# A graph network's gather-max scan: two columns a step fetched row by row into two turn buffers, instead of one and a quarter fetched into the ring

## The chip, the core and the metric

The kernel runs on one core of a Trainium2 chip. The core has five engines with a queue of instructions each: TensorE (PE), VectorE (DVE), ScalarE (ACT), GpSimd (POOL) and SyncE (SP). SyncE, ScalarE and GpSimd issue DMAs, which 16 DMA engines carry out. The metric is the device time of one execution in microseconds (us), lower is better.

## The reference, cut to what matters

Three graph layers on 6250 nodes with 200,000 edges, sorted by destination. Every layer takes, for each node, the maximum over the feature rows of its edges' sources, and projects it.

```python
def _sage_conv(x, src, dst, Wl, bl, Wr):
    agg = jax.ops.segment_max(x[src], dst, num_segments=x.shape[0])
    agg = jnp.where(jnp.isfinite(agg), agg, 0.0)
    return agg @ Wl + bl + x @ Wr
...
h = jnp.maximum(_layernorm(x, axis=-1), 0.0)
# three times, with the widths 128 -> 256 -> 256 -> 128:
h = jax.nn.leaky_relu(_sage_conv(h, src, dst, Wl, bl, Wr), 0.01)
return x + h
```

## The kernel before, in words

**Data.** The edges are cut into 512 runs of 391: 4 chains in each of 128 partitions. A *column* is one edge of one chain in all 128 partitions, 128 feature rows of w numbers (w = 128 in layer 0, 256 in layers 1 and 2). Four columns, one of each chain, are a *group*; two groups are a *block* of 8 columns; seven blocks are the *ring*, 56 columns in the on-chip memory (SBUF). A *step* is one lap of the ring. Each layer has 27 full steps (0 to 26) and a last one of 52 columns.

**GpSimd** gathers the columns: one indirect DMA each (L448), which takes 128 row numbers from `stage` and fetches 128 rows of the layer's feature table. Before each block it waits (L441, L443) until VectorE has staged that block's row numbers and until the block's old content has been written to the log.

**VectorE** (`scan_step`) runs over the groups in order: the running maximum of the last group plus a restart term goes to PSUM (a sum, L758), then the maximum of that and the gathered group goes back into the ring (L792). At the first group of each block it also copies the row numbers of the block before it, for the next lap, to `stage` (L739) and counts `block_scanned` up. At the first group of a step this is the last block's numbers, and the count tells too that the last group of the step before is no longer read.

**SyncE** (`log_step`) writes every scanned group to a log in HBM, one store a group: L1240 after `group_scanned`, L1246 after `block_scanned`. The log is gathered from at the layer's end.

**Rows.** A column that GpSimd need not gather is fetched by 128 small DMAs instead, one row each, issued by SyncE and ScalarE. The row's place in the table is a register; a portion of rows begins with one register load (TENSOR_LOAD, L321) that reads that many numbers from `row_at`. Before, 160 rows a step are fetched so: the ring's last column and 32 partitions of the one before it. GpSimd gathers that one for 96 partitions. SyncE fetches 72 in nine portions of 8 (L1231) behind its stores, ScalarE 88 in eight portions of 11 (L1155) in one go. Both wait for the store of the ring's last block, since the rows land in the ring. VectorE waits for all of them before the last group's maximum.

**ScalarE** also carries the layer's own projections (`keep_pair`, a pair of tiles a step in steps 0 to 22, two more pairs afterwards): it copies TensorE's transposed tile (L1109), loads the next tile (`h_in`, L1104), and copies TensorE's product (L1118), after the step's rows. In layer 0 it counts run ends there as well (L1125 to L1131). The order of all work is written out by hand; semaphores alone tie the queues. After a layer's scan GpSimd gathers each node's row from the log, and TensorE and VectorE project and store.

## Time and profile before

| | us |
|---|---|
| median of 3 runs (6050.76 to 6064.11) | 6052.55 |
| the profiled execution, its own time | 6050.56 |
| its span, first to last instruction | 6048.9 |
| GpSimd busy | 4524.8 (75%) |
| VectorE busy | 2893.5 (48%) |
| TensorE busy | 732.5 (12%) |
| ScalarE busy | 225.4 (4%) |
| gathers of layers 0, 1, 2: from, to | 32 to 1956, 2037 to 3958, 4044 to 5965 |

Busy times do not count DMA issues, register loads and waits, so those of SyncE and ScalarE say little about how full their queues are; the timeline shows their DMA issues (SPq, ACTq), and the view of one source line shows the register loads. "Issue" is idle time in which an engine waits for nothing that the profile shows. Releasers are inferred from semaphores.

### The profile page before, as it was taken

What the parts mean: (1) busy time and instruction counts of PE and PEld (TensorE: products, weight loads), DVE (VectorE), ACT (ScalarE), POOL (GpSimd) and SP (SyncE); (2) the same over time, 40 slices, a digit from 0 to 9 for tenths busy, and PEclk for the clock granted to TensorE, in tenths of its full rate; (3) what the DMA queues carried; (4) which work ended last, traced back from release to release, by engine and by line L of the source; (5) the groups of instructions that cost most, each with busy time, mean ns of one, the idle gap of its engine ahead of it and who ended that gap; (6) DMA issues with size and microseconds to landing.
All of it is one profiled execution on the core that took longest, in us unless ns stands there. A gap on an engine that the chain in (4) does not pass through costs nothing.

```text
span 6048.9 us, 53349 instructions
## 1 busy us (share of the span) xinstructions
PE 732.5 (12%) x2214; PEld 411.8 (7%) x2214; DVE 2893.5 (48%) x3638; ACT 225.4 (4%) x664; POOL 4524.8 (75%) x4793
## 2 busy tenths in 40 slices
PE   1111111111100311111111110040010000100003
PEld 0000000000000200000000000030000000000002
DVE  5333333333333555555555555565555555555556
ACT  1000000000000100000000000010000000000001
POOL 6777777777777777777777777767777777777776
PEclk7555555555555655555555555575555555555556
DMA  4333333333333566666666666666666666666665
GB/s 141 108 111 107 108 108 109 110 108 108 108 108 107 171 216 218 218 216 220 216 218 218 216 219 214 215 206 219 217 220 215 218 218 216 220 215 218 215 216 175
DMA packets 461123, 1089.10 MB, mean 180 GB/s; under 512 B 116295, under 2 KB 181740, under 8 KB 461068
## 3 DMA queue, kind: packets, MB, share of 16 engines
q0 software_dynamic: 203520, 519.10, 30.6%
q1 hardware_dynamic: 220508, 544.04, 24.8%
q10 hardware_dynamic: 37040, 25.45, 1.5%
q14 instruction: 48, 0.39, 0.0%
q8 instruction: 7, 0.11, 0.0%
HBM read 555.08 MB, written 533.07 MB: 180 GB/s over the span
## 4 chain that ended last, share of the span: by engine, by line
POOL 49%; issue 17%; DMA 1%; POOLq 1%; DVE 0%; PE 0%; DVEq 0%
POOL ring L448 47%; POOL ring L475 2%; POOLq L444 0%; DMA ring<-running_max_log,end_row 0%; POOLq L441 0%; DMA patch<-running_max_log,patch_row 0%; DMA ring<-features,stage 0%; DMA running_max_log<-patch 0%; POOL patch L465 0%; DVE z_sum L902 0%; DVE agg L894 0%; POOLq L455 0%; POOLq L443 0%; DMA features<-h_out 0%; DVE patch L873 0%
## 5 line engine op out<-in xcount | busy, mean ns | idle before, releaser
L448 POOL DMA_INDIRECT ring<-features,stage x4611 | 4360.0, 946 | 1432.2 <-issue 1383.7
L792 DVE TENSOR_TENSOR ring<-banks,ring 128x1024 f32<-128x1024 f32 (+1 forms) x1173 | 1227.4, 1046 | 2954.0 <-DMA ring<-features,stage 2918.9
L758 DVE TENSOR_TENSOR banks<-ring,banks 128x1024 f32<-128x1024 f32 (+1 forms) x1173 | 1232.1, 1050 | 37.5
L975 PE MATMUL banks<-wr,h_turned 128*128 128x256 f32 (+1 forms) x490 | 220.7, 596 | 3623.4 <-ACT h_turned L1109 3623.4
L975 PEld LDWEIGHTS banks<-wr,h_turned 128*128 128x128 f32 x490 | 127.2, 320 | 3687.4 <-ACT h_turned L1109 3678.6
L991 PE MATMUL banks<-dst_low,own 128*128 128x394 bf16 x200 | 100.4, 502 | 976.0 <-DVE own L734 976.0
L475 POOL DMA_INDIRECT ring<-running_max_log,end_row x147 | 142.9, 972 | 65.6 <-issue 43.9
L1109 ACT ACTIVATE h_turned<-banks 128x256 f32<-128x256 f32 (+1 forms) x147 | 51.8, 353 | 3128.6 <-issue 2664.1
L739 DVE COPY stage<-edges 128x8 int32 (+1 forms) x588 | 119.4, 203 | 88.0 <-DVE banks L758 32.8
L977 PE MATMUL banks<-b,ones 1*128 1x256 f32 (+1 forms) x294 | 157.6, 637 | 0.0
L1048 PE MATMUL banks<-wl,agg 128*128 128x256 f32 (+1 forms) x490 | 110.7, 369 | 1.2 <-DVE agg L894 0.9
L992 PE MATMUL banks<-dst_high,own 128*128 128x394 bf16 x200 | 99.1, 496 | 0.0
L991 PEld LDWEIGHTS banks<-dst_low,own 128*128 (+1 forms) x200 | 27.8, 139 | 1023.0 <-issue 1021.8
L967 PE MATMUL banks<-ident,h_in 128*128 128x128 f32 x245 | 86.6, 436 | 27.8 <-DMA h_in<-features 27.8
L1125 ACT ACTIVATE signs<-banks,node 128x391 bf16<-128x391 f32 x50 | 29.6, 592 | 1505.5 <-issue 1501.8
L1048 PEld LDWEIGHTS banks<-wl,agg 128*128 128x128 f32 x490 | 84.3, 210 | 11.1 <-DVE agg L894 4.0
L977 PEld LDWEIGHTS banks<-b,ones 1*128 1x128 f32 x294 | 72.9, 307 | 74.4 <-issue 74.4
L1175 ACT ACTIVATE agg<-zeros 128x512 f32<-128x512 f32 x75 | 47.3, 631 | 761.1 <-PE banks L1048 761.1
L1017 PE MATMUL banks<-ident,ring 128*128 128x128 f32 x20 | 5.0, 425 | 577.8 <-DVEq L804 577.8
L1036 PE MATMUL banks<-ident,ring 128*128 128x128 f32 x245 | 59.2, 319 | 62.7 <-DMA ring<-running_max_log,end_row 59.0
L1118 ACT ACTIVATE own<-banks 128x256 f32 (+3 forms) x147 | 51.1, 348 | 394.0 <-PE banks L977 394.0
L883 DVE TENSOR_SCALAR finite<-banks 128x512 int32<-128x512 int32 (+2 forms) x75 | 44.3, 591 | 42.1 <-PE banks L1036 41.2
(114 smaller groups left out, 523.4 us busy)
## 6 DMA issues: line engine op xcount, KB each, us to landing
running_max_log<-ring SPq DMA_DIRECT2D x782, 512.0 KB, 3.1
running_max_log<-ring SPq DMA_DIRECT2D x391, 256.0 KB, 2.2
ring<-features ACTq DMA_DIRECT2D x4752, 1.0 KB
ring<-features,stage POOLq DMA_INDIRECT x4611, 3.2
ring<-features SPq DMA_DIRECT2D x3888, 1.0 KB
ring<-features ACTq DMA_DIRECT2D x2376, 0.5 KB
ring<-features SPq DMA_DIRECT2D x1944, 0.5 KB
h_in<-features ACTq DMA_DIRECT2D x98, 128.0 KB, 2.5
```

What stands on the lines that cost most here:

```text
L448: pool.indirect_dma_start(ring[0:rows, c * w:(c + 1) * w], None, tables[l], bass.IndirectOffsetOnAxis(ap=stage[0:rows, b, u:u + 1].bitcast ...
L475: pool.indirect_dma_start(ring[:, t * w:(t + 1) * w], None, logs[w], bass.IndirectOffsetOnAxis(ap=end_row[:, t:t + 1].bitcast(U32), axis=0 ...
L739: dve.tensor_copy(stage[:, b, :], src_t[:, bass.ds((i + ahead) * RING_COLS + b * BLOCK_COLS, BLOCK_COLS)]).then_inc(block_scanned, 1)
L758: dve.tensor_tensor(sum_ps[:, 0:CHAINS * w].rearrange("p (h f) -> p h f", h=CHAINS), group(g - 1).rearrange("p (h f) -> p h f", h=CHAINS), ...
L792: dve.tensor_tensor(group(g), sum_ps[:, 0:CHAINS * w], group(g), ALU.max).then_inc(turn, 1)
L967: turn = pe.transpose(turn_ps[0][:, c * P:(c + 1) * P], h_in[p][:, c * P:(c + 1) * P], ident[:, :])
L975: pe.matmul(mm_ps[p][:, 0:n], h_turned[p][:, c, :], wr_sb[l][:, c, :], start=(c == 0), stop=False)
L977: pe.matmul(mm_ps[p][:, 0:n], ones[0:1, :], b_sb[l][:, :], start=False, stop=True).then_inc(own_mm, 1)
L991: pe.matmul(sel_ps[p][:, 0:RUN + 3], chosen, dst_low[:, h, :], start=(h == 0), stop=False)
L992: mm = pe.matmul(sel_ps[p][:, 0:RUN + 3], chosen, dst_high[:, h, :], start=False, stop=(h == CHAINS - 1))
L1036: turn = pe.transpose(turn_ps[b][:, t * w + c * P:t * w + (c + 1) * P], ring[:, k * w + c * P:k * w + (c + 1) * P], ident[:, :])
L1048: mm = pe.matmul(mm_ps[b][:, t * n:(t + 1) * n], agg[b][:, t * w + c * P:t * w + (c + 1) * P], wl_sb[l][:, c, :], start=(c == 0), stop=(c ...
```

## The change

- **Rows.** 256 rows a step are fetched row by row, two whole columns (`FETCHED_COLS`). They go to two new buffers, `fetched0` and `fetched1`, used in turn by step, not to the ring. GpSimd gathers 54 columns a step.
- **Shares.** SyncE fetches 128 rows in eight portions of 16, ScalarE 128 in four of 32. Both may start a step's rows once `block_scanned` says that VectorE is in the step before; the wait for the store of the last block goes. SyncE fetches portion 0 before the first store, then two after each store until all are issued.
- **Stores.** One store for a block in place of two, but in the last step of a layer.
- **Last group.** VectorE takes its maximum in two instructions: the two gathered columns first, then, after the wait for the rows, the two fetched ones.
- **ScalarE.** In layers 1 and 2 a step's own projections stand between the four portions, not behind them.
- **Loops.** VectorE, SyncE and ScalarE loop over two steps at a time, for the two buffers; step 0, and on ScalarE four steps at the end, are written out. Some semaphores are merged.

```diff
-SYNC_ROWS, SYNC_AT_ONCE = 72, 8
-ACT_AT_ONCE = 11
-ROWS = 160
+FETCHED_COLS = 2
+SYNC_ROWS = 128
+AT_ONCE, ACT_AT_ONCE = 16, 32
...
+    ROWS = FETCHED_COLS * P
...
-        return width(b, last) - (b == BLOCKS - 1 and not last)
+        return width(b, last) - (FETCHED_COLS if b == BLOCKS - 1 and not last else 0)
...
+        fetched = [sb(f"fetched{k}", [P, FETCHED_COLS * F_MAX]) for k in range(2)]
...
-                            rows = 2 * P - ROWS if c == RING_COLS - 2 and not last else P
                             pool.indirect_dma_start(
-                                ring[0:rows, c * w:(c + 1) * w], None, tables[l],
+                                ring[:, c * w:(c + 1) * w], None, tables[l],
                                 bass.IndirectOffsetOnAxis(
-                                    ap=stage[0:rows, b, u:u + 1].bitcast(U32), axis=0),
+                                    ap=stage[:, b, u:u + 1].bitcast(U32), axis=0),
                             ).then_inc(late_landed if last and b == LATE_BLOCK and u >= CHAINS else landed[b], DMA)
...
-                        elif g == GROUPS - 1:
-                            dve.wait_ge(act_rows_landed, FETCHED[1])
-                            dve.sem_inc(act_rows_landed, -FETCHED[1])
-                            dve.wait_ge(sync_rows_landed, FETCHED[0])
-                            dve.sem_inc(sync_rows_landed, -FETCHED[0])
                         dve.wait_ge(turn, carried + 2 * g + 1)
-                        dve.tensor_tensor(group(g), sum_ps[:, 0:CHAINS * w], group(g), ALU.max).then_inc(turn, 1)
+                        if g == GROUPS - 1:
+                            gathered = (CHAINS - FETCHED_COLS) * w
+                            dve.tensor_tensor(group(g)[:, 0:gathered], sum_ps[:, 0:gathered], group(g)[:, 0:gathered],
+                                              ALU.max).then_inc(turn, 1)
+                            dve.wait_ge(act_rows_landed[turn_of], FETCHED[1])
+                            dve.sem_inc(act_rows_landed[turn_of], -FETCHED[1])
+                            dve.wait_ge(sync_rows_landed[turn_of], FETCHED[0])
+                            dve.sem_inc(sync_rows_landed[turn_of], -FETCHED[0])
+                            dve.tensor_tensor(group(g)[:, gathered:CHAINS * w], sum_ps[:, gathered:CHAINS * w],
+                                              fetched[turn_of][:, 0:FETCHED_COLS * w], ALU.max).then_inc(turn, 1)
+                        else:
+                            dve.tensor_tensor(group(g), sum_ps[:, 0:CHAINS * w], group(g), ALU.max).then_inc(turn, 1)
...
-                def fetch_rows(i):
-
-                    act.wait_ge(group_scanned, i * BLOCKS + (FIRSTS * l + 1))
-                    if isinstance(i, int):
+                def rows_open(i):
+
+                    if isinstance(i, int) and i == 0:
                         act.wait_ge(rows_placed, len(widths))
-                        if l:
-                            act.wait_ge(logged[BLOCKS - 1], LOGGED[BLOCKS - 1] * l)
                     else:
-                        act.wait_ge(logged[BLOCKS - 1], i * (DMA * STORES_OF[BLOCKS - 1]) + LOGGED[BLOCKS - 1] * l)
-                    for first in range(0, ROWS_OF[1][1], ACT_AT_ONCE):
+                        act.wait_ge(block_scanned, i * BLOCKS + SIGNED * l)
+
+                def fetch_rows(i, turn_of, portions):
+
+                    for portion in portions:
+                        first = portion * ACT_AT_ONCE
                         places = row_places(1, mybir.EngineType.Activation, i, first, ACT_AT_ONCE, w)
                         for r, place in enumerate(places):
-                            act.dma_start(row_slot(1, first + r, w), table_row(l, w, place)
-                                          ).then_inc(act_rows_landed, DMA)
+                            act.dma_start(row_slot(1, turn_of, first + r, w), table_row(l, w, place)
+                                          ).then_inc(act_rows_landed[turn_of], DMA)
+
+                def step_of_rows(i, pair, turn_of):
+
+                    rows_open(i)
+                    if pair and l:
+                        for p in range(2):
+                            fetch_rows(i, turn_of, range(2 * p, 2 * p + 1))
+                            keep_turned(i, p, True)
+                            fetch_rows(i, turn_of, range(2 * p + 1, 2 * p + 2))
+                            keep_own(i, p)
+                    else:
+                        fetch_rows(i, turn_of, range(ACT_PORTIONS))
+                        if pair:
+                            keep_pair(i, 2)
 
                 load(0, 0)
                 load(1, 1)
-                fetch_rows(0)
-                keep_pair(0, 2)
-                with act.Fori(1, PAIRS - 2) as j:
-                    fetch_rows(j)
-                    keep_pair(j, 2)
-                with act.Fori(PAIRS - 2, PAIRS) as j:
-                    fetch_rows(j)
+                def two_steps(j, pair):
+
+                    step_of_rows(j * 2 + 1, pair, 1)
+                    step_of_rows(j * 2 + 2, pair, 0)
+
+                step_of_rows(0, True, 0)
+                with act.Fori(0, PAIRS // 2 - 1) as j:
+                    two_steps(j, True)
+                two_steps(PAIRS // 2 - 1, False)
                 keep_pair(PAIRS - 2, PAIR_TILES[-1])
                 keep_pair(PAIRS - 1, 0)
-                with act.Fori(PAIRS, STEPS - 1) as j:
-                    fetch_rows(j)
+                two_steps(PAIRS // 2, False)
...
-                def fetch_rows(i, g):
-
-                    first = g * SYNC_AT_ONCE
-                    if g == 0:
+                def fetch_rows(i, turn_of, portion):
+
+                    first = portion * AT_ONCE
+                    places = row_places(0, mybir.EngineType.SP, i, first, AT_ONCE, w)
+                    for r, place in enumerate(places):
+                        sp.dma_start(row_slot(0, turn_of, first + r, w), table_row(l, w, place)
+                                     ).then_inc(sync_rows_landed[turn_of], DMA)
+
+                def log_step(i, last, turn_of=0):
+                    portion, portions = 0, 0 if last else SYNC_ROWS // AT_ONCE
+                    if not last:
                         if isinstance(i, int):
                             sp.wait_ge(rows_placed, len(widths))
                             if l == 0:
@@ -1223,34 +1260,29 @@
                             else:
                                 for b in range(STORES):
                                     sp.wait_ge(h_stored[b], PER_OUT * l)
-                                sp.wait_ge(logged[BLOCKS - 1], LOGGED[BLOCKS - 1] * l)
                         else:
-                            sp.wait_ge(logged[BLOCKS - 1], i * (DMA * STORES_OF[BLOCKS - 1]) + LOGGED[BLOCKS - 1] * l)
-                    places = row_places(0, mybir.EngineType.SP, i, first, SYNC_AT_ONCE, w)
-                    for r, place in enumerate(places):
-                        sp.dma_start(row_slot(0, first + r, w), table_row(l, w, place)
-                                     ).then_inc(sync_rows_landed, DMA)
-
-                def log_step(i, last):
+                            sp.wait_ge(block_scanned, i * BLOCKS + SIGNED * l)
+                        fetch_rows(i, turn_of, portion)
+                        portion += 1
                     for b in used_blocks(last):
 
                         c, columns = b * BLOCK_COLS, width(b, last)
-                        if columns > CHAINS:
+                        if last and columns > CHAINS:
                             sp.wait_ge(group_scanned, i * BLOCKS + (FIRSTS * l + b + 1))
                             sp.dma_start(log_block(l, i, b, 0, CHAINS), ring[:, c * w:(c + CHAINS) * w]
                                          ).then_inc(logged[b], DMA)
-                            if not last and BLOCK_GROUPS * b * SYNC_AT_ONCE < SYNC_ROWS:
-                                fetch_rows(i, BLOCK_GROUPS * b)
                         sp.wait_ge(block_scanned, i * BLOCKS + (SIGNED * l + BLOCKS + b + 1))
-                        at = columns - CHAINS
-                        sp.dma_start(log_block(l, i, b, at, CHAINS), ring[:, (c + at) * w:(c + columns) * w]
+                        at = columns - CHAINS if last else 0
+                        sp.dma_start(log_block(l, i, b, at, columns - at), ring[:, (c + at) * w:(c + columns) * w]
                                      ).then_inc(logged[b], DMA)
-                        if not last and (BLOCK_GROUPS * b + 1) * SYNC_AT_ONCE < SYNC_ROWS:
-                            fetch_rows(i, BLOCK_GROUPS * b + 1)
+                        for portion in range(portion, min(portion + PORTIONS, portions)):
+                            fetch_rows(i, turn_of, portion)
+                        portion += 1
 
                 log_step(0, False)
-                with sp.Fori(1, STEPS - 1) as i:
-                    log_step(i, False)
+                with sp.Fori(0, STEPS // 2 - 1) as i:
+                    log_step(i * 2 + 1, False, 1)
+                    log_step(i * 2 + 2, False, 0)
...
```

How the instructions stand on three queues, in layer 0's loop for GpSimd and layer 1's loop for the others.

GpSimd's queue at the end of a step, before; `ring<-features,stage` is one column's gather, 128 or 96 partitions of 128 numbers.

```order
L448 DMA ring<-features,stage 128x128 [waits block_scanned,logged5]
L448 DMA ring<-features,stage 128x128 x7
L441 REGISTER_ALU
L448 DMA ring<-features,stage 128x128 [waits block_scanned,logged6]
L448 DMA ring<-features,stage 128x128 x5
L448 DMA ring<-features,stage 96x128
L455 REGISTER_ALU
```

The same place in the changed kernel.

```order
L450 DMA ring<-features,stage 128x128 [waits block_scanned,logged5]
L450 DMA ring<-features,stage 128x128 x7
L444 REGISTER_ALU
L450 DMA ring<-features,stage 128x128 [waits block_scanned,logged6]
L450 DMA ring<-features,stage 128x128 x5
L457 REGISTER_ALU
```

The gather of 96 partitions is gone, everything else stands as it stood.

SyncE's queue from the start of a step on, before; `running_max_log<-ring` is a store of a group, `ring<-features 1x1024` a row of 1024 bytes.

```order
L1240 ISA [waits group_scanned]
L1240 DMA running_max_log<-ring 128x1024
L1228 ISA
L321 ISA [waits logged6]
L321 TENSOR_LOAD row_at
L1231 DMA ring<-features 1x1024 x8
L1244 REGISTER_ALU
L1246 ISA [waits block_scanned]
L1246 DMA running_max_log<-ring 128x1024
L321 REGISTER_ALU
L321 TENSOR_LOAD row_at
L1231 DMA ring<-features 1x1024 x8
```

The same place in the changed kernel.

```order
L325 ISA [waits block_scanned]
L325 TENSOR_LOAD row_at
L1250 DMA fetched<-features 1x1024 x16
L1274 REGISTER_ALU
L1276 ISA [waits block_scanned]
L1276 DMA running_max_log<-ring 128x2048
L325 REGISTER_ALU
L325 TENSOR_LOAD row_at
L1250 DMA fetched<-features 1x1024 x16
L325 REGISTER_ALU
L325 TENSOR_LOAD row_at
L1250 DMA fetched<-features 1x1024 x16
```

A portion of 16 rows now stands ahead of the step's first store, and two stand between one store and the next.

ScalarE's queue at the end of a step's rows, before; `h_turned`, `h_in` and `own` are the own projection of a tile.

```order
L321 TENSOR_LOAD row_at
L1155 DMA ring<-features 1x1024 x11
L1108 ISA
L1109 ACTIVATE h_turned<-banks 128x256 [waits in_turned]
L1104 ISA
L1104 DMA h_in<-features 128x256
L1118 ISA [waits weights_loaded,own_mm]
L1118 ACTIVATE own<-banks 128x256
```

In the changed kernel, from the start of a step on.

```order
L325 ISA [waits block_scanned]
L325 TENSOR_LOAD row_at
L1170 DMA fetched<-features 1x1024 x32
L1122 ISA
L1123 ACTIVATE h_turned<-banks 128x256 [waits in_turned]
L1118 ISA
L1118 DMA h_in<-features 128x256
L325 REGISTER_ALU
L325 TENSOR_LOAD row_at
L1170 DMA fetched<-features 1x1024 x32
L1132 ISA [waits weights_loaded,own_mm]
L1132 ACTIVATE own<-banks 128x256
```

Between the copy of a transposed tile and the copy of its product, where ScalarE had nothing to issue but one load, a portion of 32 rows now stands.

## Rows read from the trace of the kernel before

**Rows 1.** The chain of waits that ended last, shares of the span by line.

```profile
by line: POOL ring L448 47.1%; issue 16.5%; POOL ring L475 2.1%; POOLq L444 0.2%; DMA ring<-running_max_log,end_row 0.2%; POOLq L441 0.2%; DMA patch<-running_max_log,patch_row 0.2%; DMA ring<-features,stage 0.1%; DMA running_max_log<-patch 
```

**Rows 2.** Groups by line: count, busy us, mean ns, idle us before, releasers.

```profile
L448 POOL DMA_INDIRECT ring<-features,stage x4611 | 4360.0, 946 | 1432.2 <-issue 1383.7 <-DVE stage L739 29.9 <-DMA features<-h_out 18.0
...
L792 DVE TENSOR_TENSOR ring<-banks,ring 128x1024 f32<-128x1024 f32 (+1 forms) x1173 | 1227.4, 1046 | 2954.0 <-DMA ring<-features,stage 2918.9 <-DVEq L790 15.1
```

**Rows 3.** Timeline of GpSimd over a step's end: start us, length us.

```profile
3066.12 0.95 POOL L448 DMA_INDIRECT ring<-features,stage  x1 [0.30 <-issue]
3067.38 0.92 POOL L448 DMA_INDIRECT ring<-features,stage  x1 [0.31 <-issue]
3068.59 0.96 POOL L448 DMA_INDIRECT ring<-features,stage  x1 [0.30 <-issue]
```

**Rows 4.** Timeline of SyncE's DMA issues in layer 1.

```profile
3021.25 2.52 SPq L1231 DMA_DIRECT2D ring<-features  x8
...
3049.01 0.38 SPq L1246 DMA_DIRECT2D running_max_log<-ring  x1
```

**Rows 5.** Timeline of ScalarE, a step of layer 0.

```profile
392.12 49.57 ACTq L1155 DMA_DIRECT2D ring<-features  x88
...
450.36 0.38 ACT L1118 ACTIVATE own<-banks 128x256 f32 x1 [2.55 <-PE banks L977]
```

**Rows 6.** Timeline of ScalarE, a step of layer 1.

```profile
3016.72 54.39 ACTq L1155 DMA_DIRECT2D ring<-features  x88
...
3075.02 0.38 ACT L1118 ACTIVATE own<-banks 128x256 f32 x1 [3.41 <-PE banks L977]
...
3079.33 0.38 ACT L1118 ACTIVATE own<-banks 128x256 f32 x1 [3.40 <-PE banks L977]
```

**Rows 7.** Register loads of L321, ns min/median/max: layer 0 first, then layer 1.

```profile
L321 SPq TENSOR_LOAD <-row_at x243: 969/1096/1337, 47.3 to 1875.5; - x122
L321 ACTq TENSOR_LOAD <-row_at x216: 1421/2701/3389, 46.8 to 1879.4; - x108
...
L321 SPq TENSOR_LOAD <-row_at x243: 692/1397/1947, 2050.7 to 3879.9; - x122
L321 ACTq TENSOR_LOAD <-row_at x216: 1423/3012/4004, 2050.1 to 3890.0; - x108
```

**Rows 8.** The same view of L391: GpSimd loads one register.

```profile
L391 POOLq TENSOR_LOAD <-unsorted x1: 1167/1167/1167, 27.2 to 27.2; - x1
```

**Rows 9.** The fifth register load of a ScalarE step, layer 1.

```profile
L321 ACTq TENSOR_LOAD <-row_at x1: 1442/1442/1442, 3042.9 to 3042.9; - x1
```

**Rows 10.** Timeline of VectorE from a step's last maximum on.

```profile
3073.35 1.22 DVE L792 TENSOR_TENSOR ring<-banks,ring 128x1024 f32<-128x1024 f32 x1
...
3076.00 0.17 DVE L739 COPY stage<-edges 128x8 int32 x1 [0.16 <-DVE banks L758]
...
3085.82 0.17 DVE L739 COPY stage<-edges 128x8 int32 x1 [0.16 <-DVE banks L758]
```

**Rows 11.** Groups by line and shape: the maximum at half the width.

```profile
L792 DVE TENSOR_TENSOR ring<-banks,ring 128x512 f32<-128x512 f32 x391 | 270.2, 691 | 1208.9 <-DMA ring<-features,stage 1202.2
```

**Rows 12.** Timeline of GpSimd: the first gather of block 3.

```profile
3098.63 0.95 POOL L448 DMA_INDIRECT ring<-features,stage  x1 [0.30 <-issue]
```

**Rows 13.** DMA view of 3100 to 3650 us: queues, then issues with landing us.

```profile
q0 software_dynamic: 21111, 57.40, 36.7%
q1 hardware_dynamic: 17265, 59.29, 28.8%
q10 hardware_dynamic: 3712, 2.82, 1.9%
...
running_max_log<-ring SPq DMA_DIRECT2D x112, 512.0 KB, 3.1
ring<-features ACTq DMA_DIRECT2D x704, 1.0 KB
...
h_in<-features ACTq DMA_DIRECT2D x16, 128.0 KB, 2.7
```

87 lines of the change are left out of this document (46 added, 41 removed).

## The prediction

> **What bounds the kernel now.** I read the chain of work that ended last first. It lies almost wholly on GpSimd: its gathers take 47% of the span and "issue", the time in which it waits for nothing that the profile shows, another 17% [rows 1]. The groups by line say what that is: 4611 indirect gathers of 946 ns, with 1384 of the 1432 us of idle time before them put down to issue and about 50 to VectorE and a DMA [rows 2]. VectorE, in its 1173 maxima, waits 2919 us for those gathers' data. So GpSimd runs flat out. The timeline of its queue gives the beat: a gather of 128 rows starts 1.25 us after the last one, the one of 96 rows at the end of a step is followed after 1.21 us (3067.38 to 3068.59), with gaps of 0.30 us everywhere [rows 3]. A step is thus 54 x 1.25 + 1.22, with 0.01 more at its first gather: 68.75 us, and there are 27 full steps in each of three layers. The 28th has 52 gathers and keeps them.
>
> **What the change takes off GpSimd.** One gather a step, the one of 96 rows: 3 x 27 = 81 gathers of 1.22 us, 98.8 us. A step becomes 67.53 us. The new gather order has no other difference there.
>
> **What it puts on SyncE and ScalarE.** The 128 + 128 rows that GpSimd drops are fetched one by one (160 before). They must keep under 67.5 us a step, and this decides the case.
>
> A row costs SyncE 0.32 us: eight take 2.52 us [rows 4]; I take 0.33. On ScalarE 88 rows with the seven register loads between them take 49.57 us in layer 0 and 54.39 in layer 1 [rows 5, 6]. Less seven medians of 2.70 and 3.01 us [rows 7] that is 0.349 and 0.378 us a row.
>
> The register loads ahead of rows change in size: 16 words instead of 8 on SyncE, 32 instead of 11 on ScalarE. No row shows either size. The nearest: one word 1.17 us [rows 8]; 8 words on SyncE 1.10 us median in layer 0 and 1.40 in layer 1, 0.69 at the least; 11 words on ScalarE 2.70 and 3.01, but 1.42 at the least [rows 7]. In one step the fifth load of 11 words took 1.44 us [rows 9]. ScalarE's eight loads start at words 72, 83, 94 and so on of the list; the fifth (word 116) starts at a multiple of four words and six others do not, so I put the long ones down to their start. All new portions start at multiples of 16 words. From 1 to 8 words nothing is added, from 8 to 11 at most 0.34 us, 0.11 a word. The bounds are 0.69 us and 16 x 3.01/11 = 4.4 for 16 words, 1.42 and 8.8 for 32. I take 1.6 and 2.5, near the well placed loads.
>
> SyncE: call T0 the end of VectorE's first stage copy of a step (3076.17) [rows 10]. At T0 + 9.8 the next copy (3085.82 to 3085.99) releases block 0's store. The first portion, 16 x 0.33 + 1.6, is done by T0 + 7.4, inside that wait. Then come store, two portions, store, two, store, two, store, one: seven portions of 5.4 + 1.6 us (0.1 of it between instructions), and four stores of 0.38 and some 0.15 around each, 2.1. With 2.1 us to land (128 KB of h_in take 2.7 [rows 13], and a row is 1 KB) the rows are there at T0 + 9.8 + 49.0 + 2.1 + 2.1 = T0 + 63.0. VectorE needs them late: the last maximum before T0 starts at 3073.35, 2.8 us ahead of it [rows 10], and only its second half, 0.69 us [rows 11], now reads fetched rows; so T0 + 67.5 - 2.3 = T0 + 65.2. Spare: 2.2 us; it is gone at a load of 1.9 us.
>
> Past that VectorE falls behind, SyncE no longer waits for block 0, and its cycle is all its work: 7 stores (3.7), 8 portions (43.2 + 8 loads), 2.1 to land and 2.3 on VectorE, 51.3 + 8 loads; 67.5 at a load of 2.03 us. Even then GpSimd does not stop at once. It refills block 3 at 3098.63 [rows 12], whose store was issued at 3049.01 [rows 4] and takes 3.1 us to land [rows 13]: 46 us of margin. Block 3's store goes behind seven portions now, some 12 us later in its step than before, and is twice as large (2 us at most), so some 32 us remain, per layer, before a lag costs anything; at the end of a layer VectorE, with 2.5 us a group against some 5, catches up by itself.
>
> ScalarE, layers 1 and 2: 128 x 0.378 = 48.4, four loads 10.0. The two own projections took from 3071.11, the end of the rows, to 3079.71, 8.6 us, of which 2 x 3.4 us were waits for TensorE [rows 6]; these waits now lie beside portions of rows, so 2 us stay: 60.4 of 67.5 us. Layer 0 keeps its order, with the tail from 441.69 to 450.74 [rows 5]: 44.7 + 10.0 + 9.0 + 0.5 = 64.2. ScalarE would bind at loads of 4.3 and 3.3 us. TensorE has nothing else to do there, and the wait that the interleaving adds holds only the next portion, which has the spare time above.
>
> **Edits at nothing.** One store of a block instead of two halves frees 0.5 us a block on SyncE and is counted above. The split of the last maximum adds an instruction, 2 x 0.69 for 1.22 us, on a VectorE that idles over 4 us in most blocks; if it had no idle time it would cost 0.16 x 81 = 13 us, an upper bound that I do not take. The loops of two steps and the merged semaphores issue nothing on GpSimd. Two buffers let the fetch of a step start without waiting for the ring's last store, which hides the end of the rows rather than a part of the chain: below nothing for the rows is 0 us, because the chain is GpSimd's.
>
> One DMA engine may carry every row. ScalarE's queue, q10, has 3712 packets in 550 us of layer 1 [rows 13]: 16 loads of h_in at 128 + 16 make 2304, and 1408 are left, two for each of 704 rows. So a row is one data packet and one more, not 16 pieces. The Trainium skill gives a reason ("DMA: Bandwidth & Descriptors", the section on why a DMA increments its semaphore by 16): a direct DMA picks as many engines as divide the slowest dimensions of both sides, and one that cannot be divided so uses the lowest numbered engine. By that all rows share one engine and rival C below has its place; without it they would spread, and C falls away. No view here names the engine, and the sum is the same by both.
>
> **Sum.** 6050.56 - 98.8 = 5951.8 us against the profiled execution's own time (span 6048.9 and 1.66 around it), which lies 2 us under the median of 6052.55. Forecast 5953 us.
>
> **Rivals.**
> A, partial gain: every word beyond 8 costs 0.11 us. Loads are 2.3 us for 16 words in layers 1 and 2 and 3.8 for 32. SyncE's cycle is 69.7 us, 2.2 over; 27 steps make 59, less 32 of margin: 27 us in each of two layers. ScalarE in layer 0 needs 44.7 + 15.2 + 9.5 = 69.4, 1.9 over in the 23 steps that have projections, 44 less 32: 12. Time 5953 + 66 = 6019. For it: 11 words over 8. Against it: 1 and 8 words cost the same, and ScalarE's 1.44 in layer 1 is no more than the 1.42 of layer 0.
>
> B, slower: the load costs by the word. At SyncE's 1.40/8 = 0.175 in layer 1, 16 words take 2.8 us and 32 take 5.6; SyncE's cycle is 73.7, 6.2 over, 167 less 32 = 135 us in each of two layers. Layer 0, at 1.42/11 = 0.13: ScalarE's four loads of 4.2 give 71.0, 3.5 over in 23 steps, less 32: 48. 5953 + 270 + 48 = 6271 us. It turns slower where SyncE's load passes 2.4 us: 2 x (27 x (8 x 2.4 - 16.2) - 32) = 98. For it: the loads of 11 words with a median of 3.0. Against it: one word costs no less than eight.
> A register load costs some 200 ns a register even in bulk, says the Trainium skill ("Runtime: NRT & Kernel Launch", instruction fetch mechanics). By that 16 words are an estimated 3.2 us, SyncE's cycle 76.9, 9.4 over in 27 steps of three layers, and the time about 6620 us. The trace disagrees for 8 words (1.10 in place of 1.6) and for the well placed 11 (1.44 in place of 2.2), and comes closer for the others (3.0).
>
> C, one DMA engine with all rows fills up. The three queues keep the engines 67.4% busy in layer 1 [rows 13], 46 us of a step. q10's 1.9% of 16 engines for 550 us is 167 us for 3712 packets, 45 ns each; a row is 90 ns, 256 rows 23 us. That engine would have 46 - 1 + 23 = 68 us to do in 67.5. 0.5 over in 54 steps stays within the margin; only if it needed 70 would layers 1 and 2 lose 2 x (27 x 2.5 - 32) = 71 us: 6024. Against it: most of q10's bytes are in the larger packets, so a row's real share is under the mean.
>
> **Chances.** The forecast 0.72, A 0.11, B 0.08 and the page's form of it 0.04, C 0.05. The forecast's own range is 5944 to 5965; the 8 in 10 reach to A: 5944 to 6024. A change under 0.2%, 12 us, could not be told from none. Faster: the forecast and most of A and C, 0.84; the same 0.03; slower 0.13.
>
> **What would show it.** GpSimd: 4530 gathers of 946 ns, a start every 1.25 us, steps of 67.5 us, and idle time still put down to issue. Register loads of about 1.6 us on SyncE and 2.5 on ScalarE. VectorE: the second half of the last maximum starts without a wait for rows, or after one under 3 us. Wrong would be: loads over 2.05 us on SyncE, VectorE waiting for a features row in step after step with growing length, and GpSimd's first gather of a block waiting for a store (logged) or a stage copy.

## The result

The changed kernel takes **6317.38 us** (median of 4 runs, 6316.51 to 6318.04) beside 6052.94 us of the kernel before: ratio 1.0433, 95% interval [1.0415, 1.0451]. It is slower by 264 us; I had forecast 5953, faster by 99. The profiled execution took 6317.91 us with a span of 6316.2. The experiments below ran in five sets, each beside the kernel before, which took 6051 to 6052 us in three of them and 7859 and 7864 us in the other two (e5 to e8, and h1 and h2), where everything was slower and only the ratios within a set can be read.

GpSimd's first and last gather of a layer and its mean step (steps 6 to 26), read from its timeline:

| layer | before | after | step before | step after |
|---|---|---|---|---|
| 0 | 1922.4 us | 1891.6 us | 68.78 us | 67.63 us |
| 1 | 1920.0 us | 2072.7 us | 68.75 us | 75.17 us |
| 2 | 1920.0 us | 2058.4 us | 68.75 us | 74.19 us |

Layer 0 gained 30.8 us of the 32.9 forecast (27 gathers of 1.22 us). The wide layers lost 152.7 and 138.4. These and 7 us between and behind the layers make the span's 267 us.

**The groups by line** of the changed kernel (count, busy us, mean ns of one, idle us before and its releaser) answer to [rows 2, 11]:

```profile
L450 POOL DMA_INDIRECT ring<-features,stage x4530 | 4295.0, 948 | 1758.6 <-issue 1716.8
L800 DVE TENSOR_TENSOR ring<-banks,ring 128x1024 f32<-128x1024 f32 (+1 forms) x1092 | 1143.0, 1047 | 1561.8 <-DMA ring<-features,stage 1542.4
...
L797 DVE TENSOR_TENSOR ring<-banks,fetched 128x512 f32<-128x512 f32 (+1 forms) x81 | 48.7, 601 | 1683.3 <-DVEq L796 1683.2
```

The gathers are as many and as long as forecast, but GpSimd idles 326 us more. VectorE waits 1683 us ahead of the half maximum that reads fetched rows; L796 is its wait for SyncE's rows. Since GpSimd's idle time is all called "issue", its timeline must say where it stands (start us, length, idle before):

```profile
3135.48 0.95 POOL L450 DMA_INDIRECT ring<-features,stage  x1 [0.30 <-issue]
3142.33 0.95 POOL L450 DMA_INDIRECT ring<-features,stage  x1 [5.91 <-issue]
```

The second is the first gather of block 3. In layers 1 and 2 it comes 6 us late on the mean, for the store of block 3 (the first of block 2 another 1 us). SyncE's queue in the same step shows when that store goes out (start, length, count):

```profile
3079.15 5.18 SPq L1250 DMA_DIRECT2D fetched<-features  x16
3084.60 0.38 SPq L1276 DMA_DIRECT2D running_max_log<-ring  x1
3088.37 12.08 SPq L1250 DMA_DIRECT2D fetched<-features  x32
3100.72 0.38 SPq L1276 DMA_DIRECT2D running_max_log<-ring  x1
...
3132.46 0.38 SPq L1276 DMA_DIRECT2D running_max_log<-ring  x1
3136.24 5.09 SPq L1250 DMA_DIRECT2D fetched<-features  x16
3141.59 7.94 SPq L1276 DMA_DIRECT2D running_max_log<-ring  x3
3157.70 5.30 SPq L1250 DMA_DIRECT2D fetched<-features  x16
```

Block 3's store is issued at 3132.46. The DMA view of 3125 to 3145 us gives 9.2 us to landing (median of three), that is about 3141.7; the gather follows at 3142.33. Nothing in this queue waits for a block until the last of the three stores at the end: SyncE is saturated, as the prediction's "past that" had it. It stands still in three kinds of places. Behind each block store 3.4 us pass before the first row (3084.98 to 3088.37): that is the register load. Its durations over the step (ns min/median/max):

```profile
L325 SPq TENSOR_LOAD <-row_at x8: 1194/3088/4534, 3074.5 to 3132.9; - x8
```

Between block 6's store at 3149.20 and the next row at 3157.70 lie the jump back of the loop (5.0 us behind the branch, without a wait) and a load. And the last row is issued at 3141.33, but VectorE's half maximum starts only at 3146.70:

```profile
3146.70 0.69 DVE L797 TENSOR_TENSOR ring<-banks,fetched 128x512 f32<-128x512 f32 x1 [32.53 <-DVEq L796]
...
3148.85 0.17 DVE L741 COPY stage<-edges 128x8 int32 x1 [0.20 <-DVE banks L760]
```

**The DMA view** of steps 6 to 26 of layer 2 (4620 to 6000 us), which answers to [rows 13]:

```profile
q0 software_dynamic: 48150, 131.54, 31.8%
q1 hardware_dynamic: 23619, 139.83, 27.3%
q10 hardware_dynamic: 9544, 6.81, 1.9%
...
running_max_log<-ring SPq DMA_DIRECT2D x131, 1024.0 KB, 6.2
```

A store of twice the size lands after 6.2 us in place of 3.1.

### The profile page after: what moved, and what is told of

It is laid out like the page before. It is cut to its first block and busy times, and to the rows that moved or that the text cites. A ratio compares the mean times of both kernels' runs of the same rounds, so it can differ in the third digit from the quotient of the medians.

```text
span 6316.2 us, 65405 instructions
## 1 busy us (share of the span) xinstructions
PE 703.7 (11%) x2214; PEld 401.6 (6%) x2214; DVE 2877.7 (46%) x3719; ACT 227.0 (4%) x664; POOL 4458.9 (71%) x4712
## 5 line engine op out<-in xcount | busy, mean ns | idle before, releaser
L450 POOL DMA_INDIRECT ring<-features,stage x4530 | 4295.0, 948 | 1758.6 <-issue 1716.8
L800 DVE TENSOR_TENSOR ring<-banks,ring 128x1024 f32<-128x1024 f32 (+1 forms) x1092 | 1143.0, 1047 | 1561.8 <-DMA ring<-features,stage 1542.4
L797 DVE TENSOR_TENSOR ring<-banks,fetched 128x512 f32<-128x512 f32 (+1 forms) x81 | 48.7, 601 | 1683.3 <-DVEq L796 1683.2
L1132 ACT ACTIVATE own<-banks 128x256 f32 (+3 forms) x147 | 51.3, 349 | 1442.1 <-issue 1326.3
```

Source lines behind the costliest of these rows:

```text
L450: pool.indirect_dma_start(ring[:, c * w:(c + 1) * w], None, tables[l], bass.IndirectOffsetOnAxis(ap=stage[:, b, u:u + 1].bitcast(U32), axi ...
L800: dve.tensor_tensor(group(g), sum_ps[:, 0:CHAINS * w], group(g), ALU.max).then_inc(turn, 1)
```

## The experiments

Eighteen runs of fourteen kernels follow; f5 to f8 are the same kernels as e5 to e8, run again in another set. Letters are sets, numbers kernels.

What the traces of the sets with 6051 to 6052 us say of SyncE's queue, in us per step, mean of steps 6 to 26 of layer 2. "Jump" is the pause behind the branch, spread over the two steps of the loop. "Last row" is from the end of its issue to the start of VectorE's half maximum; "landing" is the median of a 1 MB store in the DMA view of 4620 to 6000 us:

| kernel | time | step | 8 loads | jump | wait for block 6 | last row | store landing |
|---|---|---|---|---|---|---|---|
| changed | 6317 | 74.2 | 19.5 | 2.3 | 4.3 | 3.3 | 6.2 |
| e1 written out | 6251 | 73.4 | 19.8 | 0 | 7.9 | 6.4 | 9.3 |
| e2 load ahead | 6259 | 73.3 | 10.7 | 2.5 | 7.9 | 6.9 | 8.1 |
| e3 half stores | 6384 | 76.7 | 18.4 | 3.2 | 0 | 1.3 | 4.9 (512 KB) |
| e4 loads of 32 | 6324 | 75.1 | 16.3 | 2.4 | 8.2 | 8.8 | 11.5 |
| f6 a step ahead | 6283 | 73.1 | 20.3 | 3.0 | 0 | no wait | none given |
| f7 both ahead | 6282 | 72.8 | 12.1 | 3.1 | 0 | no wait | 18.6 |
| f5 e2, other rows | 6090 | 69.8 | 11.6 | 3.4 | 2.6 | 1.6 | 4.5 |
| g4 f7, other rows | 6082 | 69.7 | 12.0 | 3.1 | 0 | no wait | 4.7 |

(e4 has four loads. The expectations below give 7.7 us for e2's last row; its mean is 6.9, in turn some 5.6 and 8.4.)

**e1: the loop written out.**

```diff
...
-                with sp.Fori(0, STEPS // 2 - 1) as i:
+                for i in range(STEPS // 2 - 1):
...
```

> The changed kernel with SyncE's loop of two steps written out, so that SyncE never jumps back inside a layer; all else is as in the change. In the changed kernel SyncE stands still for 4.3 us behind each jump back in layers 1 and 2, that is 2.2 to 2.3 us a step. Theory L (SyncE's cycle of 74.2 us in layers 1 and 2 sets the step, and each microsecond of it costs 54 us): the cycle falls to 71.9 and the time from 6317 to about 6195 us. Rival F (the code must be fetched anyway and comes no faster in straight line): the pauses turn up elsewhere in SyncE's queue and the time stays at 6317. Rival D (the rows' landing or ScalarE's rows set the step): 6317 as well, with the pauses gone.

Measured 6251.22 us, ratio 1.0329 [1.0312, 1.0346]: 66 us less than the changed kernel, half of what theory L gave. The pauses went (F falls), so the jump did cost. But the last row now landed 6.4 us after its issue in place of 3.3. Most of what SyncE gained, the landing took.

**e2: the load ahead of the store.**

```diff
...
+                        ahead = load_places(i, portion) if portion < portions else None
                         sp.wait_ge(block_scanned, i * BLOCKS + (SIGNED * l + BLOCKS + b + 1))
...
-                            fetch_rows(i, turn_of, portion)
+                            fetch_rows(i, turn_of, portion, ahead)
...
```

> The changed kernel, where SyncE loads the 16 places of the first portion behind each block store before it waits for that block, so that the load stands ahead of the store and the rows follow the store at once. Four of the five loads a step that stand right behind a store are moved; there they take 3.15 us in layers 1 and 2 and elsewhere 1.20. Theory L with the load as the victim: 4 x 1.95 = 7.8 us a step go, SyncE's cycle falls from 74.2 to 66.4 us, under GpSimd's 67.5, and the time to about 5960 us. Rival Q (the 1 MB store holds the whole queue for 2 us): the first row behind the store waits in place of the load, and the time stays at 6317. Rival W (loads cost by the word, wherever they stand): the moved loads still take 2.4 to 3.1 us, 6317.

Measured 6259.36 us, 1.0342 [1.0325, 1.036]. The moved loads took 1.20 us, so W falls; with it falls rival B of the prediction, though its 6271 us was near. Of the 8.8 us saved in loads 4.1 came back as longer DMAs, mostly the third and fourth row behind a store (0.78 and 0.49 in place of 0.23 us), so Q holds in part. Most of the rest went into the landing, 6.9 us in place of 3.3. In the DMA view of 5111.3 to 5114.0 us of this kernel, when the store issued at 5107.51 has left the other engines:

```profile
q0 software_dynamic: 182, 0.49, 58.5%
q1 hardware_dynamic: 15, 0.02, 3.8%
q10 hardware_dynamic: 12, 0.01, 0.8%
```

In the 2 us before, q1 had 101.9% of 16 engines. Now it has 3.8%, six tenths of one engine, in packets of 8 KB that still trail in at one or two a microsecond, and the rows behind them stand.

**e3: half stores.**

```diff
...
-                        if last and columns > CHAINS:
+                        if columns > CHAINS:
...
+                            if portion < portions:
+                                fetch_rows(i, turn_of, portion)
+                                portion += 1
...
```

> The changed kernel with the stores of the kernel before: each block goes out as two stores of a group, 512 KB in layers 1 and 2, each as soon as its group is scanned, with one portion of 16 rows behind each until the eight are out. All eight loads then stand behind a store or nearly so. If the extra time of a load goes with the bytes of the store ahead of it (2.14 us behind 512 KB in layer 0 of the changed kernel): 8 x 2.14 = 17.1 in place of 19.5 us, with four more stores of 0.5 us in the rows' way: cycle 73.8, time about 6295 us. If a store of any size costs a load 2 us: 8 x 3.15 = 25.2, cycle 81.9, time 6730. If it is the block store alone that hurts and a load behind a group's store takes the 1.35 us of the kernel before: 10.8, cycle 67.5, time about 5960.

Measured 6384.40 us, 1.0547 [1.0529, 1.0564]. Loads took 2.3 us each, near the 2.14 of the first estimate (behind a 512 KB store) and far from the 3.15 of the second and the 1.35 of the third. I had reckoned with four more stores in the rows' way; SyncE, which never waits here, has all seven more of a step to do, its own work is 76.7 us, and the landing is short.

**e4: loads of 32 words.**

```diff
-AT_ONCE, ACT_AT_ONCE = 16, 32
+AT_ONCE, ACT_AT_ONCE = 32, 32
...
-    PORTIONS = 2
+    PORTIONS = 1
```

> The changed kernel with SyncE's rows in four portions of 32 in place of eight of 16, in the same order of rows and stores: one portion first and one behind each of the first three block stores. ScalarE's loads of 32 words take 2.2 us at the median. If the store ahead adds a fixed 2 us: 3 x 4.2 and one of about 3.2 make 15.8 in place of 19.5 us a step; cycle 70.5, time about 6120 us. If the time behind a store grows by the word (3.15/16 each): 3 x 6.3 + 4.2 = 23.1, cycle 77.8, time about 6510. A load by the word everywhere (16 words 1.2, 32 words 2.4) and +2 behind a store is the first of these within 0.6 us.

Measured 6323.86 us, 1.0451 [1.0433, 1.0468], not the 6120 of the fixed surcharge, though its loads, all behind stores, took 4.3 us at the median (4.1 on the mean), near the 4.2 that it says. The 3.2 us saved were again lost in the landing, 8.8 us. After four kernels it looked as if something beside SyncE's queue held the step near 73 us.

**f6 and f7: rows a step ahead**, f7 with e2's load ahead as well.

```diff
...
-                        fetch_rows(i, turn_of, portion)
+                        fetch_rows(i + 1, turn_of, portion)
...
```

> The changed kernel, where SyncE fetches the rows of the next step between the block stores of this one (the second buffer is free by then), and those of a layer's first step ahead of everything. Loads, stores, rows and loops are as in the change. Theory L (the cycle is closed through the rows: last row of a step, landing 3.2 us, VectorE's last maximum and copy 2.5 us, block store, next step's rows): 5.7 us leave the cycle of 74.2, SyncE's own work of 68.5 us stays, and the time falls to about 6010 us, at best 5965. Rival H (the engine that carries the rows is the bound, not SyncE's order): its backlog stays, block 3's store still lands late and GpSimd waits for it: 6200 to 6260.

> The one before with the register load ahead of the block store as well. Theory L: SyncE's work is 60.7 us of 67.5 and GpSimd alone sets the step: about 5955 us. Rival H (the engine that carries the rows): 6200 to 6260, as without the load ahead.

First run (e6, e7): 9070.43 and 9080.55 us beside 7858.86, ratios 1.155 and 1.155. Run again (f6, f7): 6282.53 us, 1.0383 [1.0366, 1.0401], and 6281.95 us, 1.0379 [1.0362, 1.0397]. Theory L fails: VectorE no longer waits for rows, the loop through the landing is open, and 8 us less in loads change nothing. The step stays at 73. H's range, 6200 to 6260, is missed as well, by 22 us. SyncE's queue is full in both: it waits for no block, and the loop's jump, 3.0 and 3.1 us a step, is still there. From f6 to f7 its DMA issues grow from 34.0 to 41.8 us a step, which is just what the loads gave back. They are held up, by up to 3.9 us (ns min/median/max), most of all the first row behind a store (1.06 us on the mean), and a block store lands after 18.6:

```profile
L1254 SPq DMA_DIRECT2D fetched<-features x2433: 227/228/3891, 4619.7 to 5998.9; - x188
```

```profile
q0 software_dynamic: 49126, 134.18, 32.4%
q1 hardware_dynamic: 24034, 141.99, 27.8%
q10 hardware_dynamic: 9551, 6.79, 2.1%
...
running_max_log<-ring SPq DMA_DIRECT2D x133, 1024.0 KB, 18.6
```

The 16 engines are 62% busy on average, yet a store takes three times as long as in the changed kernel. If one engine carries all rows, the packet records sum up for it as follows, per step of 72.8 us: a sixteenth of the gathers 23.1, of the stores 19.1, of the rest 1.5; 128 rows of SyncE 14.3, 128 of ScalarE 8.3, their semaphore packets 2.5; together 68.8 us, 95%. In f6 it is 95% too, in the changed kernel 85%, in the kernel before 81%, in layer 0 of the changed kernel 50%. These sums hold the stretch that crowding gives a packet. With the 46 and 9 ns that a row's two packets take when nothing is in their way, the same work in f7 would be an estimated 58 us, 80%.

The packet records name no engine, but they have starts and durations, and these show that it is one (steps 6 to 26 of layer 2 of the changed kernel). No two of SyncE's 2560 row packets overlap by more than 1 ns. None of ScalarE's 2213 row packets outside the loads of `h_in` overlaps one of SyncE's by more than 10 ns; were one list shifted by 0.15 to 1 us, 423 to 663 would. And while one of SyncE's row packets is in flight, 16 packets of 2 KB or more never are (0 of 2560 cases), though 1 us later they are in 323 cases, and in 22% of all time. So the rows of both queues take turns on one of the 16 engines, and a sixteenth of the stores and gathers goes through it too.

**f5 and g4: half of the rows off that engine**, on the base of e2 and of f7.

```diff
...
-                        for r, place in enumerate(places):
-                            act.dma_start(row_slot(1, turn_of, first + r, w), table_row(l, w, place)
...
+                        act.dma_start(fetched[turn_of][first:first + ACT_AT_ONCE, 0:w],
+                                      tables[l][first:first + ACT_AT_ONCE, :]
...
```

Both kernels leave out what ScalarE's rows are for: a fourth of the last group is computed from other rows.

> The kernel with the load ahead of the store (6259 us), where ScalarE fetches its 128 rows with four DMAs of 32 neighbouring rows from the head of the table: the same bytes, the same register loads, but spread over the DMA engines and without 124 of its 128 DMAs a step. Those are not the rows that the edges name, so that a fourth of the last group is computed from other rows. With the load ahead SyncE's issuing ended 8 us a step earlier, yet the step stayed at 73.3 us, because the last rows landed 7.7 us after their issue in place of 3.1; during each block store 1 to 3 store packets a microsecond trail behind the others. Theory H (one DMA engine carries all rows, falls behind in each block store, and SyncE's rows wait there behind the store's share): without ScalarE's rows the engine has about a third less of that to do, the landing falls to 4 or 5 us and the time to 6060 to 6120 us. Rival S (the rows wait only for the store ahead of them in their own queue, whoever else uses the engine): no change, 6259.

> The kernel with rows a step ahead and the load ahead of the store (6282 us, 72.8 us a step in layers 1 and 2), where ScalarE's 128 rows are four DMAs of 32 neighbouring rows, so that a fourth of the last group is computed from other rows. Theory H (the one engine with all rows is full: in 72.8 us its share of gathers and stores takes 43 us and the rows' packets about 30): 128 rows less free some 15 us, nothing is over GpSimd's 67.5 us in layers 1 and 2, and the time is 5965 us (layer 0 starts 17 us late in this kernel). Rival Q (SyncE's own queue is the bound, 72 to 73 us whoever else fetches): 6250 to 6280.

First run (e5): 8302.69 us, 1.0563. Run again (f5): 6090.39 us, 1.0068 [1.0051, 1.0084], within H's 6060 to 6120 and 169 us under e2, where S had no change. g4: 6082.30 us, 1.0051 [1.0034, 1.0068], 200 us under f7, where Q had none. In g4 stores land after 4.7 us in place of 18.6:

```profile
q0 software_dynamic: 51453, 140.57, 33.4%
q1 hardware_dynamic: 26139, 152.71, 28.9%
q10 hardware_dynamic: 7632, 6.17, 1.5%
...
running_max_log<-ring SPq DMA_DIRECT2D x138, 1024.0 KB, 4.7
```

More bytes are moved in the same time, and the assumed engine's sum is 51.6 us, 74%. H gave g4 5965 us, though. The 117 us that are missing are SyncE's own queue: it never waits, and its work is 69.7 us, since behind the stores the DMAs of rows are slow even here (38.8 us of DMA issues a step in place of the 32.4 of the changed kernel). Both kernels also issue 124 DMAs fewer on ScalarE; no run keeps that number and moves the rows to other engines, so the two effects are not parted.

**e8, f8, g1, g2, g3: rows in pieces.**

```diff
...
+            return in_pieces(fetched[turn_of][p:p + 1, 0:FETCHED_COLS * w].bitcast(U8))[:, :, c, :]
...
```

(This is g1 to g3. In e8 and f8 the four pieces of a row lie side by side.)

> The kernel with the load ahead of the store (6259 us), where every row is described as four pieces of 256 bytes (128 in layer 0), on both queues, so that a DMA can be divided over four engines. The Trainium skill says that a direct DMA takes as many engines as divide the slowest dimensions of both sides (DMA: Bandwidth & Descriptors, the section on the increment by 16). Theory H: the load of the rows is spread, the last rows land 3 to 5 us after their issue in place of 7.7, time 6060 to 6120 us. Rival I (four pieces cost the issuing queue more: at 0.05 us a row 6.4 us a step): no gain or slower, 6250 to 6600. Rival S (the queue's own order): the landing stays at 7.7 us and the time at 6259.

> The same base (6282 us), all 256 rows fetched as asked, but each written as two halves of 512 bytes that lie apart in the buffer, so that they can't be merged into one piece and a DMA can be divided over two engines; VectorE's last half of a maximum reads the halves in order. Theory H: each of two engines has the rows' packets at half their bytes; a row is then about 30 in place of 55 ns undisturbed and the engines are at 60 us of 67.5: time 5965 to 6000 us. Rival I (a DMA in two pieces costs the issuing queue more, say 0.05 us a row): SyncE 66 + 6 us, ScalarE over 67.5: 6100 to 6250. Rival N (both pieces go to one engine, which then has twice the packets): slower than 6282, 6400 or more.

> As the one before, with four pieces of 256 bytes. Theory H: four engines share the rows; 5965 to 6000 us, no better than two unless two were still over. Rival I: 0.1 us more a row in place of 0.05, 6400 or more. Rival N: four times the packets on one engine, 7000 or more.

> The changed kernel itself (6317 us) with each row in two pieces that lie apart, and nothing else. Theory H and L together: the last rows land 2 us after their issue in place of 3.2 and the row-carrying engine is no bound, but SyncE's cycle, closed through its loads behind the stores, its jumps back and VectorE, stays at some 73 us: 6220 to 6260 us. If the engine alone were the cause: 5960. If it were none: 6317.

e8 took 9006.28 us (1.147), f8 6258.55 us, 1.0342 [1.0324, 1.0359], just e2's time. Its row packets were still of 1024 bytes: the pieces had been merged, so the run says nothing on H. In g1 to g3 the pieces lay apart, and packets of one queue's rows do overlap there, two in g1 and up to four in g3: the pieces went to two and four engines, so rival N falls. g1 took 10089.38 us (1.667), g3 10084.36 (1.667), g2 10288.48 (1.700). Rival I had the direction, but 0.05 us a row was far off (ns min/median/max of SyncE's row DMAs in 10 us of g1):

```profile
L1263 SPq DMA_DIRECT2D fetched<-features x12: 562/624/644, 5299.7 to 5309.3; - x12
```

A row in pieces costs the issuing queue 0.62 us in place of 0.23, whether two or four. That cost hides what the engine's relief gives, which could not be tried in this way.

**h1 and h2: fewer rows in the wide layers.**

```diff
...
+COLS_OF = ((2, 2), (1, 2), (1, 2))
...
```

(h2 has `((2, 2), (1, 1), (1, 1))`.)

> The changed kernel with the load ahead of the store and fewer rows in layers 1 and 2: odd steps fetch two columns (256 rows), even steps one (128), each divided in halves between SyncE and ScalarE; GpSimd gathers 54 and 55 times in turn, in loops of two steps. The engine that carries the rows then needs 43 us for gathers and stores and 0.116 us for each of 192 rows, 65 us of a mean step of 68.1; SyncE's queue has 96 rows a step, some 55 us. Theory H with the ledger: no step waits for a block store, layer 0 gains 31 us on the kernel before and layers 1 and 2 some 16 each: 5989 us. Rival R (a step of 256 rows overruns before the light one relieves it): GpSimd still waits at block 3 in odd steps, up to 5 us in each of 26: 5990 to 6120.

> The same kernel with two columns in every step of layer 0 and one (128 rows, 64 and 64) in every step of layers 1 and 2: 55 gathers of 128 rows there, 68.76 us a step as in the kernel before. Theory H: 6052 - 31 = 6021 us. If loops of two steps or the block stores cost something by themselves in layers 1 and 2, it shows as more than 6030.

They took 8616.21 and 8237.38 us beside 7864.41, ratios 1.0956 [1.092, 1.0992] and 1.0472 [1.0438, 1.0506]. Fewer rows lose less (e6 had 1.155), but whether either beats the kernel before where that takes 6051 us stays open; no version here was shown to do so.

## Why the prediction was wrong

**GpSimd's side: right.** 4530 gathers of 948 ns, 1.25 us apart, 67.63 us a step in layer 0, and 30.8 us gained there.

**ScalarE: right.** Its rows cost 0.35 to 0.37 us, its loads 2.2 us at the median (I took 2.5; the first of a step took 5.4 to 5.6 in the wide layers), and in layers 1 and 2 a step's last row was out some 80 us, a whole step, ahead of SyncE's. It never set the step. That 32 well placed words took less than the 2.70 and 3.01 us of 11 badly placed ones fits my reading of the start; no run tests it.

**SyncE's register loads: the size was off, and the cause that I gave for it.** I took 1.6 us and put the spare at 0.4. A load of 16 words takes 1.20 us where rows stand ahead of it, but some 2.1 right behind a store of 512 KB and 3.2 behind one of 1 MB. Five of eight stand there (the one behind the jump takes 1.2 all the same, its counterpart in the other step 4.5 to 5.0), so the mean is 2.44, over the 2.03 at which I had the queue saturate. In layer 0, where stores are half as large, it is 1.73, under the 1.9 that the spare allowed, and layer 0 gained. The step that failed is "One store of a block instead of two halves frees 0.5 us a block on SyncE": I counted the issue of the larger store and not what stands behind it. In [rows 7] the sign was there, 1.10 us in layer 0 and 1.40 in layer 1, where stores are twice as large; I took it for a cost by the word, in rival B, and not for one of the store ahead. The number of words does matter behind a store: 8 words behind 512 KB took 1.4 us in the kernel before, 16 take 2.1. Rival B came near in time by a mechanism that e2 refutes.

**The loop of two steps: not at nothing.** "The loops of two steps and the merged semaphores issue nothing on GpSimd" was true and beside the point: SyncE's body grew from 72 to 256 rows, and each jump back cost 4.6 us (mean of layer 1; 4.7 in layer 2) in place of 0.2 before. The Trainium skill has the rule that I should have weighed ("Runtime: NRT & Kernel Launch", instruction fetch mechanics): a taken branch out of the fetched window stalls until its target has been fetched. The trace agrees, and e1 shows it: without jumps the pauses are gone.

**The landing of rows: 3.3 us in place of 2.1.** With these three the prediction's own formula for SyncE's cycle closes in layer 2: 51.3 + 8 x 2.44 + 2.3 + 1.2 = 74.3 us; measured 74.2. It was the right formula with wrong entries.

**The margin of 32 us: too large.** Layer 2 lost 170 us on its forecast length (2058.4 against 27 x 67.53 + 52 x 1.25 = 1888) where 27 x 6.66 = 180 were over: 10 us of margin (22 by the same sum in layer 1). Of the store of block 3 I had said that its size adds "2 us at most" to the 3.1 us of its landing; it took 9.2 us in the step shown.

**Rival C, to which I gave 0.05, named a deeper cause, though not as I had it.** Its sum was 68 us for the one engine in a step of 67.5, and "only if it needed 70" would it cost. In the changed kernel the engine has 63 us of work in 74.2, so it is not full. f7 is free of the late loads and of the loop through the landing, though not of the jump, and stands at 72.8 with that engine at 95% by the packet records. f5 and g4 take half of the rows away and gain 169 and 200 us. What I missed is that an engine need not be full on average: each 1 MB store gives it 64 KB in a lump, SyncE's rows stand behind that in the same queue, and so do block 3's last packets, for which GpSimd waits. "A row's real share is under the mean" was right in the changed kernel (58 ns for q10's packets of 1 KB, 69 for SyncE's rows, and some 10 for the second packet, against 90 for both). It is wrong under the load of f7 (112 ns on the mean for SyncE's rows).

The causes lie in layers, not side by side. By the forecast 5953 us were to be had; no run reached that. SyncE's own queue, jumps and slow issues behind stores included, costs up to 6082 (g4). ScalarE's rows on the shared engine take it to 6282 (f7). The late loads and the loop closed through the landing take it to 6317. That is why e1, e2 and e4 each took away a true cost of 2 to 9 us a step and got 66, 58 and nothing. The shares hold in this order of removal; no run takes the rows off the engine in the changed kernel itself.

That all rows lie on one engine is read from the packet times above and from the trailing packets. The Trainium skill's rule on how many engines a DMA takes ("DMA: Bandwidth & Descriptors", the section on the increment by 16) says the same. What is open: a resource shared by both issuing queues, relieved by the 124 DMAs that f5 and g4 do not issue, would explain their gain as well, though not why the landing of stores grows to 18.6 us.

## What to carry to other kernels

When an order of stores and small DMAs in one queue is changed, what stands right behind the large store is part of its price, and it grows with the store's bytes. Many one-row DMAs add up on one DMA engine (95% in f7) while the average of 16 looks idle (62%): add up that engine's share of everything, and leave room for the lump of each large store. Where removing a measured cost gives back less than it measured, look for what became longer instead; in e1, e2 and e4 it was mostly one number, the time from the last issue to its consumer.

## What the runs showed of the hardware

- A TENSOR_LOAD of 16 words on SyncE takes 1.20 us, of 32 words about 2.2 on ScalarE; the load of 16 takes 2.1 to 2.3 us right behind a 512 KB store and 3.2 behind 1 MB (32 words: 4.3). Moved ahead of the store it takes 1.20 again, and nearly half of the difference reappears in the DMAs behind the store.
- A loop whose body has some 600 instructions on SyncE pauses 3.6 us (layer 0) to 4.7 us (layer 2) at each jump back in the changed kernel, and some 6.5 us in the wide layers of e3, where no wait stands ahead of the jump; one of some 220 instructions (the kernel before) pauses 0.2 us.
- A DMA of one row in two or four separate pieces takes 0.62 us to issue (g1, g3), in one piece 0.23.
- Row packets of both issuing queues take turns on one DMA engine: 0 of 2213 of ScalarE's overlap one of SyncE's by more than 10 ns (changed kernel). A 1 KB row packet takes 46 ns undisturbed and 112 on the mean in f7.
- Where the kernel before took 7859 and 7864 us, SyncE's and ScalarE's queues stop for 0.70 or 1.39 us between instructions. In h2, 25% of SyncE's gaps between a register move and its DMA are over 0.6 us (4200 to 5900 us), in the changed kernel none is; GpSimd's gathers keep their 1.25 us. SyncE's register moves in e6 and, below, in f6, the same kernel (ns min/median/max):

```profile
L1250 SPq MOVE fetched<-features x1428: 2/29/1397, 4620.3 to 5783.0; - x179
```

```profile
L1250 SPq MOVE fetched<-features x2402: 29/29/38, 4620.1 to 5995.9; - x185
```

The cause of that was not found.
